# One token chunk of the experts moved from layer 0's scans of the next image to layer 1's scans, which go by halves too

## The reference, cut to what matters

```python
# layer 0: 4 directions x 384 channels x 16 states, over L = 1024 tokens
h = h * exp(dt * A) + dt * u * B          # per channel and state
y = sum over states of h * C
x = x + gelu(layernorm(merge of the 4 y))
t = t + ffn(layernorm(t))                 # factored weights
# layer 1: 1 direction x 768 channels x 16 states
x = x + layernorm(out_proj((scan(xin) + xin * D) * silu(z)))
masked = softmax(gate), kept for the best 2 of 4 experts, normalised
for e in range(4):                        # un = layernorm(t)
    t = t + masked[e] * (gelu(un @ w1[e] + b1[e]) @ w2[e] + b2[e])
```

## Time and profile before

| what | value |
|---|---|
| median of 3 runs | 6349.33 us (6349.22 to 6351.49) |
| profiled execution | 6345.9 us, span of its records 6344.1 us |
| layer 0's scans of image 0 | 44 to 693 us |
| layer 1's scans, whole lanes | four stages of 350 us |
| fused scans with experts | three stages of 913 to 914 us |
| behind the last of layer 1's scans | 5827 to 6344 us: `out_projection`, two layer norms, the last image's experts |

### The profile page before, as it was taken

One profiled execution on the slowest core, in us unless ns is written; L12 is line 12 of the kernel. 1 busy time (PEld: TensorE's weight loads), 2 busy tenths in 40 slices (PEclk: granted clock), 3 DMA queues, 4 the chain that ended last, 5 costly groups with the idle time before them and its releaser, 6 DMA issues. The chain is left out here.

```text
span 6344.1 us, 55727 instructions
## 1 busy us (share of the span) xinstructions
PE 5366.4 (85%) x16384; PEld 3105.2 (49%) x16384; DVE 4736.0 (75%) x4348; ACT 3244.2 (51%) x4562; POOL 4003.7 (63%) x2455
## 2 busy tenths in 40 slices
PE   6777777789999976778999987677999998767899
PEld 2222242256666633235666654223666664422777
DVE  7999769667777857956777875994777776697544
ACT  3433433257777743327777764333777775332222
POOL 6999449547777727926777761991777775396121
PEclk8888888889999988889999998888999999888999
DMA  5555134247667604416677650541667673342110
GB/s 195 210 210 209 65 140 153 97 155 249 232 241 244 220 29 181 154 54 235 224 244 238 234 176 35 207 156 67 234 238 246 229 252 112 120 156 104 53 45 33
DMA packets 334477, 1058.94 MB, mean 167 GB/s; under 512 B 30754, under 2 KB 120866, under 8 KB 324936
## 3 DMA queue, kind: packets, MB, share of 16 engines
q1 hardware_dynamic: 334152, 1055.17, 47.5%
HBM read 1046.13 MB, written 8.91 MB: 166 GB/s over the span
## 5 line engine op out<-in xcount | busy, mean ns | idle before, releaser
L402 PE MATMUL banks<-prod,ident 128*128 128x512 f32 x1944 | 1158.3, 739 | 611.3 <-DVE prod L544 482.6
L402 PEld LDWEIGHTS banks<-prod,ident 128*128 128x128 f32 x1944 | 403.5, 226 | 1359.3 <-DVE prod L544 843.1
L951 POOL TENSOR_TENSOR h<-du,Bb 128x512 f32<-128x512 f32 x768 | 972.6, 1283 | 134.6 <-DVE banks L993 108.6
L535 DVE TENSOR_TENSOR_SCAN banks<-banks,h 128x1024 f32<-128x1024 f32 x396 | 906.7, 2290 | 58.5 <-POOL h L500 55.5
L893 ACT ACTIVATE banks<-delta,A 128x512 f32<-128x512 f32 x1152 | 775.7, 684 | 222.3 <-DVE prod L1002 154.4
L797 PE MATMUL banks<-prod,ident 128*128 128x512 f32 x1584 | 818.3, 600 | 70.6 <-DVE prod L1002 49.2
L808 PE MATMUL banks<-big,w 128*128 128x256 f32 x3456 | 839.4, 382 | 0.1
L821 PE MATMUL banks<-Cb,w 128*128 128x256 f32 x3456 | 834.5, 380 | 0.0
L808 PEld LDWEIGHTS banks<-big,w 128*128 128x128 f32 x3456 | 654.9, 191 | 292.2 <-issue 218.8
L821 PEld LDWEIGHTS banks<-Cb,w 128*128 128x128 f32 x3456 | 653.2, 190 | 266.8 <-issue 176.3
L960 POOL TENSOR_TENSOR h<-h,C 128x512 f32<-128x512 f32 x360 | 460.4, 1279 | 506.8 <-ACT carry L878 332.2
(11 more groups left out here) (262 smaller groups left out, 8871.9 us busy)
## 6 DMA issues: line engine op xcount, KB each, us to landing
w<-w_in SPq DMA_DIRECT2D x384, 576.0 KB, 5.7
Bb<-half_rows SPq DMA_DIRECT2D x384, 512.0 KB, 4.6
Bb<-rows SPq DMA_DIRECT2D x288, 512.0 KB, 4.1
Cb<-rows SPq DMA_DIRECT2D x288, 512.0 KB, 3.8
C<-half_rows SPq DMA_DIRECT2D x192, 512.0 KB, 7.0
Cb<-half_rows SPq DMA_DIRECT2D x192, 512.0 KB, 5.0
C_first<-rows SPq DMA_DIRECT2D x32, 1024.0 KB, 8.0
C_a<-rows SPq DMA_DIRECT2D x24, 1024.0 KB, 8.1
```

What stands on the lines that cost most here:

```text
L402: mm = eng.matmul(ps[:, c, :], m.ident[:, :], src[:, cols(c)], start=n == 0, stop=added(s) == (i + 1) * N, skip_group_check=True)
L535: eng.tensor_tensor_scan(flip(to), flip(slot(s)), flip(m.dBu[:, s % DRIVES, :]), 0.0, ALU.mult, ALU.add).then_inc(st.scanned, 1)
L951: eng.tensor_tensor(m.dBu[:, s % DRIVES, :], m.du[:, i % 2, :], m.B[b % BRING][:, cols(s % 2)], ALU.mult).then_inc(st.dbu, 1)
```

## The change

`fused_scans` becomes general: number of tiles per half (`tiles`), the list of guest chunks (`guests`, where a chunk lies in the working tensors and where in the image), the pair spacing (`every`), an optional next image, an optional weight load ahead. Layer 0's stage has three guest chunks with a pair every 36/7 steps (72 pairs). The fourth chunk's x, un and expert rows are copied aside by POOL in `routing` (`late`), and its 24 pairs run in layer 1's scans of the next image, a pair every 15/2 steps. Layer 1's scans use the same function: 6 tiles by two halves, 12 lanes, 192 steps. Image 0's layer 1 scans have no guest. `w_out` has a buffer of its own and is loaded at the stage's start. The loop now has two iterations, and one more image is written out behind it.

```diff
-def fused_scans(p, m, g, st, directions, rows, out, following, turn):
+def fused_scans(p, m, g, st, directions, tiles, rows, guests, every, out, following=None, turn=None, load_ahead=None):
-    TILES = CT
+    TILES = tiles
-    UNITS = (L // QUARTER) * E * PER
+    UNITS = len(guests) * E * PER
     def pair_at(v):
-        return v * 31 // 8
+        return v * every[0] // every[1]
-    LAST = pair_at(UNITS // 2 - 1) + 12
+    LAST = max(STEPS, pair_at(UNITS // 2 - 1) + 12)
     def chunk(k):
-        return slice(k // E * QUARTER, (k // E + 1) * QUARTER)
+        return guests[k // E][0]
             def exchange(q):
-                at = slice(q * QUARTER, (q + 1) * QUARTER)
+                here, there = guests[q]
                 eng.wait_ge(st.accumulated, (q + 1) * E)
-                eng.dma_start(out[:, :, at], m.x[:, :, at]).then_inc(st.sent, 16)
+                eng.dma_start(out[:, :, there], g.x[:, :, here]).then_inc(st.sent, 16)
                 eng.wait_ge(st.sent, 16 * (q + 1))
-                eng.dma_start(m.x[:, :, at], following[:, :, at]).then_inc(st.reloaded, 16)
+                if following is not None:
+                    eng.dma_start(m.x[:, :, there], following[:, :, there]).then_inc(st.reloaded, 16)
...
+            if following is not None:
+                for there in range(len(guests) * QUARTER, L, QUARTER):
+                    at = slice(there, there + QUARTER)
+                    eng.dma_start(m.x[:, :, at], following[:, :, at]).then_inc(st.reloaded, 16)
+            if load_ahead is not None:
+                load_ahead(eng, st.ahead)
...
-def routing(p, m, g, st):
+def routing(p, m, g, late, st):
...
+        @block.gpsimd
+        def _(eng):
+            rest = slice(L - QUARTER, L)
+            eng.tensor_copy(late.x[:, :, :], m.x[:, :, rest]).then_inc(st.aside, 1)
+            eng.tensor_copy(late.un[:, :, :], g.un[:, :, rest]).then_inc(st.aside, 1)
+            for e in range(E):
+                eng.wait_ge(st.row_taken, (e + 1) * NH)
+                eng.tensor_copy(late.row[:, e, :], g.row[:, e, rest]).then_inc(st.aside, 1)
...
                 with ExitStack() as scans:
-                    ms = scan_tensors(scans, name)
-                    w_out = ms.C[:, 0:CT, :].rearrange("p k l -> p (k l)")[:, 0:DT1 * C]
+                    ms = half_scan_tensors(scans, name)
+                    g = Named(late, **expert_tensors(scans, name))
+                    w_out = tensors(nc, scans, [(f"w_out_{name}", [P, DT1, C], F32)])[f"w_out_{name}"]
...
-                    lane_scans(p, ms, s_scan, mamba, lanes, rows,
-                               load_ahead=lambda eng, done: eng.dma_start(w_out, p.io["w_out"]).then_inc(done, 16))
+                    guests = [] if before is None else [(slice(0, QUARTER), slice(L - QUARTER, L))]
+                    fused_scans(p, ms, g, s_fused, mamba, DT1, half_rows, guests, (15, 2), before,
+                                load_ahead=lambda eng, done: eng.dma_start(w_out[:, :, :], p.io["w_out"]).then_inc(done, 16))
...
+                    guests = [(slice(q, q + QUARTER), slice(q, q + QUARTER)) for q in range(0, L - QUARTER, QUARTER)]
+                    fused_scans(p, half_scan_tensors(fused, name + "0"), g, s_fused, directions, CT, half_rows, guests, (36, 7),
+                                out, following=following, turn=(u, ut))
...
-            with nc.Fori(0, B - 1) as b:
-                from_scans("a", following=io["x"][b + 1])
...
-            from_scans("b")
+            from_scans("first", late, following=io["x"][1])
+            with nc.Fori(0, B - 2) as b:
+                image("a", out[b], io["x"][b + 1])
+                from_scans("a", late, before=out[b], following=io["x"][b + 2])
+            image("b", out[B - 2], io["x"][B - 1])
+            from_scans("b", late, before=out[B - 2])
```

More of the change, by code:

```diff
@@ L27 @@
 P = 128
+QUARTER = 256
 B, C, HH, WW = 4, 384, 32, 32
@@ L731, in _ @@
             load_b(1)
-            load_w1(0)
-            load_w2(0)
+            if guests:
+                load_w1(0)
+                load_w2(0)
             load_c(0, 1)
             load_b(2)
-            load_w1(1)
-            load_w2(1)
-            for s in range(max(STEPS, LAST + 8)):
+            if guests:
+                load_w1(1)
+                load_w2(1)
+            if following is not None:
[4 more added lines that the diff above has]
+                load_ahead(eng, st.ahead)
+            for s in range(LAST + 8):
                 i, n = s // N, s % N
@@ L762, in _ @@
                         exchange(k // E)
-            eng.wait_ge(st.reloaded, 16 * (L // QUARTER))
+            if following is not None:
+                eng.wait_ge(st.reloaded, 16 * (L // QUARTER))
+            if load_ahead is not None:
+                eng.wait_ge(st.ahead, 16)
         @block.tensor
@@ L826, in _ @@
             dt_product(0)
-            for s in range(max(STEPS, LAST)):
+            for s in range(LAST):
                 i, n = s // N, s % N
@@ L891, in decay @@
                 x, j, _ = lane(i)
-                a = x.a_at + n * CT + j
-                eng.activation(slot(s), m.delta[:, i % 2, :], ACT.Exp, scale=m.A0[:, a:a + 1]).then_inc(st.decay, 1)
+                eng.activation(slot(s), m.delta[:, i % 2, :], ACT.Exp, scale=x.A(j, n)).then_inc(st.decay, 1)
             def gelu(u):
@@ L912, in _ @@
                     decay(s)
-                    if n == 14 and i < TILES:
+                    if turn is not None and n == 14 and i < TILES:
                         u, ut = turn
@@ L1023, in accumulate @@
                 eng.wait_ge(st.evicted, (k + 1) * CT)
-                eng.tensor_tensor(m.x[:, :, chunk(k)], m.x[:, :, chunk(k)], g.tmp[:, :, :],
+                eng.tensor_tensor(g.x[:, :, chunk(k)], g.x[:, :, chunk(k)], g.tmp[:, :, :],
                                   ALU.add).then_inc(st.accumulated, 1)
             delta(0)
-            for s in range(max(STEPS, LAST)):
+            for s in range(LAST):
                 i, n = s // N, s % N
@@ new lines, in to_scans @@
+                with ExitStack() as route:
+                    made = tensors(nc, route, [
+                        (f"probs_{name}", [P, TT, E], F32), (f"rank_{name}", [P, TT, E], F32),
+                        (f"comb_{name}", [P, TT, E], F32), (f"t1_{name}", [P, TT], F32), (f"t2_{name}", [P, TT], F32)])
+                    named = {key[:-len(name) - 1]: t for key, t in made.items()}
+                    routing(p, m, Named(un=un, row=g.row, diag=m.prod[:, 0, :].rearrange("p (t n) -> p t n", n=P),
+                                        ones=m.prod[:, 1, 0:P], **named), late, s_route)
@@ L1860, in build, with scans @@
+            def scans(name, g, out, following):
+                with ExitStack() as fused:
+                    g = Named(g, un=un, x=m.x, **expert_tensors(fused, name + "0"))
                     order = [(0, take_first), (2, take_more), (1, take_turned), (3, take_turned)]
```

72 lines of the change are left out of this document (42 added, 30 removed).

## The result

The changed kernel took 6454.19 us (median of 4 runs, 6441.31 to 6456.0), the kernel before 6349.27 us beside it (4 runs, 6348.51 to 6351.49). The ratio is 1.016, with a 95% interval from 1.0143 to 1.0178: the change makes the kernel slower by 105 us. The prediction said 6158 us and gave 0.87 to "faster". It had the sign wrong, and its range ended at 6300 us. The profiled execution took 6456.0 us, with a span of 6454.2.

What follows compares the result with a forecast made beforehand. PE's matmuls were taken to bound the fused scans, DVE layer 1's scans. Terms -339 + 24 + 129 + 1 - 6 = -191 us took the profiled 6345.9 to 6155, plus 3.4 to the median: 6158 us; range 6050 to 6300.

Steps and rivals of the forecast that it cites:

- part 1: Layer 0's stage: 48 of 192 units leave, 124 us of PE; stage 800 us, three stages -339 us.
- part 3: Layer 1's scans with 24 guest pairs for three images: 393 us a stage, three stages +129 us.
- -375.5 + 288w: Whole kernel: change in time, -375.5 us without any DVE wait, plus w us for each of 288 pairs.
- B: Both scan stages: DVE's wait stays 1.18 us a pair; stages 836 and 409 us, total 6314 us; chance 0.19.
- C: ACT's in-order gelu blocks hold the scans: DVE idleness stays, stages 895 and 428 us, total 6548 us; chance 0.06.
- D: Layer 0's stage: PE, idle more often, drops its clock; at 0.85 the total is 6530 us; chance 0.05.
- A: Both scan stages: engines overlap better than forecast, 775 and 383 us with guests, total 6049 us; chance 0.16.
- The prediction's estimate by that rule: ACT's gelu block: a drain with each table load makes it 6.2 us instead of 3.4; total near 6260 us.
- The loop: Hardware loop's jumps back: two become one, sparing DVE idleness, -6 us.

Runs made afterwards that it cites:

- The copies by POOL: Changed kernel, with POOL instead of ACT copying the last column of the states POOL holds, before its product: 6348.64 us.
- the later chain: Changed kernel, kept columns still on ACT, with gelus, downs and evictions one step later: 6314.45 us.
- both: Changed kernel, with POOL copying its own kept columns and gelus, downs and evictions one step later: 6256.5 us.
- one and both in the kernel before: Kernel before, with POOL copying its own kept columns: 6332.0 us; with gelus, downs and evictions one step later as well: 6419.82 us.
- the filler: Changed kernel, with one more matmul of zeros after each add without an up or down beside it, in layer 1's guest stages: 6438.14 us.
- the fastest kernel: Changed kernel, POOL copying its own kept columns, gelus and downs one step later in layer 0, two in layer 1, evictions at s+11 in both: 6193.84 us.
- later evictions: Changed kernel, with POOL copying its own kept columns and evictions at s+10 instead of s+9: 6292.87 us.

## Why the prediction was wrong

**The step that failed** is the size of what DVE waits per pair, w. The prediction sized it twice: "I add 11 us to 789" in part 1 and "half the present 1.18 us a pair, 0.52" in part 3. With the prediction's own sums without any wait, 751 and 380.5 us, the measured stages give w = (863 - 751) / 72 = 1.55 us in layer 0's and (432.8 - 380.5) / 24 = 2.18 in layer 1's, 1.71 on average. The prediction took 0.65 and put the break-even at 1.30. Its formula, -375.5 + 288w, gives +117 us for 1.71; the span grew by 110. So the sum was right but for one number, and that number had the sign in it.

One part of the error is plain bookkeeping: the present w was more than 1.18. That figure left out the two rows shown above; with them it is (113.2 + 16.3 + 10.3) / 96 = 1.46, already above the break-even. And the prediction's own sums give more still: the stage before is 751 us and four more evictions, 761, without any wait, and it took 913, so w was 152 / 96 = 1.58. In layer 0's stage w did not fall at all, from 1.58 to 1.55. The traces say the same: DVE's gaps of more than 0.15 us between first and last scan sum to 158 us for 96 pairs before and 118 us for 72 after, 1.65 and 1.63 us a pair. With w merely kept, the formula gives -375.5 + 288 x 1.58 = +80 us. The rest of the 110 is layer 1's 2.18.

The other part is that I took the waits to go away with PE's load. In the earlier trace rows ACT waited 103 us for ups. I took this for PE's shortage, which would go with PE's load. Part of it did. The rest was order: from an up to its gelu there is one step, whatever PE's mean load is, and in that step PE also has two downs, an add and at times a `dt` product. Part 3 compared a block of 3.4 us with 5.5 us of decays in hand. But the block is 5.1 us or more when the up is late, and POOL has no such stock: it stood behind the block for its column, and the drives behind POOL. A smaller third, in layer 0's stage, is the eviction's distance from the last down. The copies by POOL (105.5 us), the later chain (140) and both (198) show the first two, and the runs with one and both in the kernel before, 16 us gained and 71 lost, show that they are causes in the changed kernel and not a general loss.

Two slips in the prediction's sums weigh little. Half of 1.18 is 0.59 and not 0.52, 5 us in all. And layer 1's stage with guests is built on 370 us, the one without on 374; it measured 370.9. Its own test named the right side: it said that a fused stage above 835 us with DVE waits over 1.2 us a pair, and not a clock under 0.95, would mean B or C, and the stage had 863 us, 1.55 and 0.97.

**The stage table misled in one more way.** PE's 764 us of busy time plus 25 of idleness "as now" was not a bound that holds by itself: PE was hardly idle before because it was far behind. The relief was also smaller than forecast: PE's busy time fell by 100 us, from 888 to 788, and not by 124, at a clock of 0.97. With POOL's copies and the later chain or evictions it is 770 to 774 at 0.99, so some 15 us of PE's time a stage came with the waiting and the lower clock. No run tells which of the two led.

**The rivals.** C (each gelu block holds the scans) is what happened: the place was right, its point of decision (w = 1.35) was passed. Its 6548 was too high, though all the old idleness per pair did stay: its 193 us came from busy times and held 41 us (748 - 707, in the prediction's own check) of gaps that the 706 us of lanes have in them already. Without these it is w = 1.58 and 6429 us, 25 under the result. Its chance of 0.06 was the error in the chances. What I set against it, that PE's shortage makes most of the idleness, may hold for the kernel before, where POOL's copies only moved the waits; in the changed kernel other waits took its place. B (1.18 us a pair stays) was too low, since the present w was more than 1.18. D (the clock) has a share in single blocks: in the three windows here, of the changed kernel, the clock is 0.67 and 0.65 just ahead of the late up at 2511.5 and 1.00 beside it.

```profile
2496.00:2501.00 5.00, 3.94 (x5) 1.30 (x6) 4.73 (x6) 2.72 (x7) 4.37 (x4) 0.67 0.03 12
2501.00:2506.00 5.00, 5.00 (x11) 2.55 (x10) 4.73 (x6) 1.70 (x5) 4.98 (x5) 0.65 0.47 171
2506.00:2512.00 6.00, 6.00 (x24) 4.28 (x23) 3.91 (x5) 3.60 (x7) 0.54 (x1) 1.00 0.55 151
```

What it costs in the whole is not isolated: the filler's 16 us are net of the PE time that it takes itself. But layer 1's stage fell from 433 to 405 us with the copies and the later chain while its mean clock went from 0.93 to 0.94, so most of that loss is not the clock. A (6049) is refuted: even the fastest kernel here has stages of 807.5 and 403 us where A had 775 and 383.

**The table loads.** In the changed kernel too a load begins where the gelus end: 2511.59 + 0.84 = 2512.43, and the load is at 2512.44. The Trainium skill, page "ScalarE: Activation LUTs", section "What ACT_TABLE_LOAD costs", states a drain with each load. The rows show none: before each of the 576 loads of the 288 pairs at most 0.02 us are empty, and behind each load back to exp 0.01. The prediction's estimate by that rule, 6260 us, is nearer to the result than its forecast, but the loss was in the waits.

**What held.** DVE's durations: in the stage without a guest the lanes take 28.6 to 31.3 us from take to take, for the 29.4 predicted. The first scan comes 12.8 to 13.1 us after layer 1's start (14 predicted), the stage without a guest is 370.9 (374). The counts of an up's records are 864 and 288 a stage. `out_projection` and all behind it keep their times. The loop gave 12 us instead of 6: from the end of layer 0's scans to the start of layer 1's, the two jumps before lie in 160.5 and 159.8 us against 153.7 behind the loop. The jump of the changed kernel lies elsewhere, between layer 1's scans and the next layer 0's, and is not to be seen there: 119.6 us, where the kernel before has 119.8 and 120.3 without a jump.

**Left open.** The fastest kernel still has w = (807.5 - 751) / 72 = 0.78 in layer 0's stage and (403.3 - 380.5) / 24 = 0.95 in layer 1's. What these consist of wasn't taken apart. Nor is it shown by a run why one step more costs the kernel before 88 us against its copies alone. And later evictions alone were not run in the kernel before, where DVE waits 31.5 us a stage at that place, so its best variant may be better than the 6332.0 us of POOL's copies.

## What to carry to other kernels

When work is taken off the engine that sets the pace, look at each wait in its shadow and ask whether it comes from that engine's load or from the order in which instructions stand; only the first kind goes away. For each in-order engine that runs ahead, count how many steps lie between the producer's place and the consumer's place as the clock sees them, with the consumer's lead taken off, and look for the smallest result that stands behind its longest block, here one column of 128 values worth 105 us. A change that loses may be good with its order set anew: this one lost 1.6%, and with its copies and its later chain it is 2.4% faster than the kernel before and 2.2% faster than the kernel before with POOL's copies (6332.0), the best variant of that kernel that was run.

## What the runs showed of the hardware

A copy of one column of 128 values costs POOL 0.20 us (60 of them, 12.2 us, in a stage) and ACT 0.15 to 0.20, so such a copy can go wherever its consumer is. The jump back of the hardware loop cost about 6 us of DVE's time in front of layer 1's stage and nothing visible when it stood in front of layer 0's. In a stage of 433 us of which PE was busy 356 the mean granted clock was 0.93, and with the filler, 384 of 431 us, 0.96. Last, removing ACT's 737 us of table loads gave 142 us in the changed kernel and 56 us once a copy of 12 us a stage was moved: what an operation is worth depends on what stands behind it.
